# The causal mask of one attention sublayer, added in blocks of 32 queries

## The reference

```python
q = (x @ Wq + bq).reshape(B, T, H, D).transpose(0, 2, 1, 3)
k = x @ Wk + bk
v = x @ Wv + bv
q = apply_rope(q)
k = apply_rope(k)
att = jnp.einsum('bhqd,bkd->bhqk', q, k) / jnp.sqrt(jnp.float32(D))
causal = jnp.tril(jnp.ones((T, T), dtype=bool))
att = jnp.where(causal[None, None], att, jnp.float32(-jnp.inf))
att = jax.nn.softmax(att, axis=-1)
out = jnp.einsum('bhqk,bkd->bhqd', att, v)
out = out.transpose(0, 2, 1, 3).reshape(B, T, C)
return out @ Wo + bo
```

## Time and profile before

| what | value |
|---|---|
| median of three runs | 1877.55 us (1872.98 to 1877.91) |
| the profiled execution | 1875.85 us |
| its span in the trace | 1874.1 us |
| TensorE busy over the span | 1541.5 us |
| DVE, ScalarE, GpSimd busy | 1112.2, 875.0, 611.7 us |

### The profile page before, as it was taken

The page is one execution under the profiler, slowest core; times in us unless marked ns, Lnnn a source line. Parts: engine busy times, 40 slices in busy tenths (PEclk is TensorE's granted clock), DMA queues, the critical chain, the costliest instruction groups (busy, mean ns, idle before and its releaser), DMA issues.

```text
span 1874.1 us, 42923 instructions
## 1 busy us (share of the span) xinstructions
PE 1541.5 (82%) x15916; PEld 1011.6 (54%) x15916; DVE 1112.2 (59%) x3614; ACT 875.0 (47%) x2556; POOL 611.7 (33%) x849
## 2 busy tenths in 40 slices
PE   4556379979989778898889633799799999998998
PEld 3334246546656555455557422566477777776443
DVE  3434555556757557116757687466566666664776
ACT  2222334445556335434546544344366666666443
POOL 1422231222226434002212243112144444443666
PEclk6555569989999889999989855799899999999999
DMA  5000000000000000000020000000000000000000
GB/s 229 2 1 2 1 1 2 2 1 2 2 2 2 1 0 1 1 1 2 2 117 3 24 1 1 1 2 2 24 1 1 0 0 0 0 0 1 1 12 12
DMA packets 3605, 21.53 MB, mean 11 GB/s; under 512 B 1129, under 2 KB 1385, under 8 KB 2025
## 3 DMA queue, kind: packets, MB, share of 16 engines
q1 hardware_dynamic: 3434, 19.22, 2.7%
HBM read 18.15 MB, written 1.05 MB: 10 GB/s over the span
## 4 chain that ended last, share of the span: by engine, by line
PE 67%; DVE 11%; issue 7%; ACT 6%; POOL 4%; DVEq 3%; POOLq 1%; DMA 0%; ACTq 0%; SPq 0%
PE ps L707 5%; PE ps L646 5%; PE ps L675 5%; PE ps L2829 4%; PE ps L2478 4%; PE ps L2488 3%; PE ps L2502 3%; PE ps L2457 3%; PE ps L2464 3%; PE ps L606 2%; PE ps L717 2%; PE ps L2301 2%; PE ps L1264 2%; PE ps L662 2%; PE ps L694 2%
## 5 line engine op out<-in xcount | busy, mean ns | idle before, releaser
L894 DVE TENSOR_REDUCE arena<-ps 128x4 f32<-128x512 f32 x320 | 204.3, 684 | 132.5 <-PE ps L662 74.8
L832 ACT ACTIVATE arena<-ps 128x512 f32<-128x512 f32 x320 | 171.7, 596 | 126.6 <-PE ps L694 124.2
L537 POOL TENSOR_TENSOR arena<-arena,C 128x512 f32<-128x512 f32 x80 | 83.2, 1041 | 420.2 <-ACT arena L853 138.6
L2394 POOL TENSOR_TENSOR arena<-arena 128x512 f32<-128x512 f32 x128 | 132.9, 1044 | 224.2 <-DVE arena L2703 223.8
L1264 PE MATMUL ps<-hid,WA 128*20 128x16 f32 x1024 | 56.8, 196 | 88.0 <-DVE hid L1315 88.0
L2621 ACT COPY arena<-ps 128x512 f32<-128x512 f32 x128 | 69.1, 589 | 122.9 <-PE ps L2488 122.9
L2612 ACT ACTIVATE arena<-ps,arena 128x256 f32<-128x256 f32 x256 | 120.1, 479 | 11.8 <-issue 8.1
L2829 PE MATMUL ps<-WA,maskadd 128*128 128x512 f32 x256 | 119.8, 598 | 1.8 <-DVE arena L2972 1.8
L707 PE MATMUL ps<-arena 128*32 128x128 f32 x2560 | 110.9, 282 | 3.3 <-ACT arena L832 3.0
L646 PE MATMUL ps<-arena 32*128 32x128 f32 x2560 | 104.1, 288 | 9.9 <-POOL arena L537 6.8
L2695 DVE TENSOR_REDUCE arena<-ps 128x2 f32<-128x512 f32 x128 | 82.5, 686 | 45.0 <-PE ps L2478 43.5
(11 more groups left out here) (455 smaller groups left out, 3847.8 us busy)
## 6 DMA issues: line engine op xcount, KB each, us to landing
WA<-w_late SPq DMA_DIRECT2D x1, 4228.0 KB, 13.7
WA<-w_early SPq DMA_DIRECT2D x1, 1600.0 KB
R<-rows SPq DMA_DIRECT2D x1, 1282.0 KB, 6.8
WB<-w_rest SPq DMA_DIRECT2D x1, 1152.0 KB, 10.1
xT_all<-x_T SPq DMA_DIRECT2D x1, 1024.0 KB, 6.4
x_all<-x_tok SPq DMA_DIRECT2D x1, 1024.0 KB, 12.2
arena<-mask SPq DMA_DIRECT2D x1, 1024.0 KB
ctxT_all<-ctx_T SPq DMA_DIRECT2D x1, 1024.0 KB
```

The costliest lines, as they stand in the source:

```text
L537: nc.gpsimd.tensor_tensor(heads(v_(n % 2, ATT, "P", WIDE_Q, 512)), src.unsqueeze(1).broadcast_to([128, 4, 128]), cst("tilemask").unsqueeze ...
L832: nc.scalar.activation(v_(s, ATT, "PT", 512 * t, 512), ps[s][t][:, :], ACT.Exp, scale=SCALE).then_inc(pT_sb, 1)
L894: nc.vector.tensor_reduce(v_(z, ATT, "m", 4 * t, 4), heads(ps[z][t][:, :]), AXX, ALU.max)
L2394: nc.gpsimd.tensor_tensor(p, p, v_(z, LAT, "rec", 4 * u + 2 * x, 2).unsqueeze(2).broadcast_to([128, 2, 256]), ALU.mult).then_inc(l_sub, 1)
```

## The change

For `mask_kind == "causal"` the mask is added by products of 32 rows instead of 128. Two new tiles, `causal_4` and `ident_4`, hold the mask and the identity so that each group of 32 rows of the array has all four blocks of 32 queries. They are filled by 32 transfers on SyncE's queue from `causal_b` and `ident_b`, after the last load. In `scores`, block b covers the keys from 32 b on. The order of blocks is outside and that of row groups inside, and `s_ps` is incremented in block 3. In `scores_T`, block b covers the 32 queries of the block for all keys.

```diff
+        causal_4 = sb("causal_4", [128, 4, 128], BF16)
+        ident_4 = sb("ident_4", [128, 4, 128], BF16)
...
+        const_cast = sem("const_cast")
+        fours_in = sem("fours_in")
...
+                elif mask_kind == "causal":
+                    if n == 0:
+                        pe.wait_ge(fours_in, 512)
+                    for b in range(4):
+                        for t in ORDER:
+                            mm = nc.tensor.matmul(heads(ps[z][t][:, :])[:, :, 32 * b:128], ident_4[rows(t), b, :],
+                                                  causal_4[rows(t), b, 32 * b:128].unsqueeze(1).broadcast_to(
+                                                      [32, 4, 128 - 32 * b]), start=False, stop=b == 3,
+                                                  skip_group_check=True)
+                            if b == 3:
+                                mm.then_inc(s_ps, 1)
                 elif mask_kind is not None:
                     for t in ORDER:
-                        r = (maskadd[:, n:n + 1, :].broadcast_to([128, 4, 128])
-                             if mask_kind == "full" else causal_b[:, :].unsqueeze(1).broadcast_to([128, 4, 128]))
-                        nc.tensor.matmul(heads(ps[z][t][:, :]), ident_b[:, :], r, start=False, stop=True,
+                        nc.tensor.matmul(heads(ps[z][t][:, :]), ident_b[:, :],
+                                         maskadd[:, n:n + 1, :].broadcast_to([128, 4, 128]), start=False, stop=True,
                                          skip_group_check=True).then_inc(s_ps, 1)
...
+                elif mask_kind == "causal":
+                    for b in range(4):
+                        for t in T_ORDER:
+                            nc.tensor.matmul(heads(ps[s][t][:, :])[:, :, 32 * b:32 * b + 32], causal_4[rows(t), b, :],
+                                             ident_b[rows(t), rows(t)].unsqueeze(1).broadcast_to([32, 4, 32]),
+                                             start=False, stop=False, skip_group_check=True)
                 elif mask_kind is not None:
-                    l = causal_b[:, :] if mask_kind == "causal" else maskadd[:, n, :]
                     for t in T_ORDER:
-                        nc.tensor.matmul(heads(ps[s][t][:, :]), l,
+                        nc.tensor.matmul(heads(ps[s][t][:, :]), maskadd[:, n, :],
                                          ident_b[:, :].unsqueeze(1).broadcast_to([128, 4, 128]), start=False,
                                          stop=False, skip_group_check=True)
...
+            sp.wait_ge(const_cast, 1)
+            for t in range(4):
+                for b in range(4):
+                    to, of = slice(32 * t, 32 * t + 32), slice(32 * b, 32 * b + 32)
+                    sp.dma_start(causal_4[to, b, :], causal_b[of, :]).then_inc(fours_in, 16)
+                    sp.dma_start(ident_4[to, b, :], ident_b[of, :]).then_inc(fours_in, 16)
...
-            nc.vector.tensor_copy(negrow_b[:, :], cst("second").broadcast_to([128, REG_ROWS]))
+            nc.vector.tensor_copy(negrow_b[:, :], cst("second").broadcast_to([128, REG_ROWS])).then_inc(const_cast, 1)
```

## The result

The changed kernel takes 1858.89 us, the median of 4 runs (1855.54 to 1860.48), where the kernel before takes 1875.65 us (1872.98 to 1877.91). The ratio is 0.9906, with a 95% interval of 0.9893 to 0.9919: 16.8 us less. The profiled execution took 1860.04 us, its span is 1858.1 us. The functions of the sublayer stand some lines lower in this file: scores L650 (was L646), their mask L667 (L662), transposed scores L689 (L675), their mask L699 (L685), fold L713 (L694), values L726 (L707), maxima L913 (L894), rope L903 (L884), widening L541 (L537).

A forecast was written before the change was run, and what follows sets the result against it. TensorE was taken to bound the causal sublayer until a loop through DVE and POOL closes at 7.41 us. Savings of 14 x 1.07 + 1.0 + 0.8 = 16.8 us from 1877.55 gave 1861 us, range 1856 to 1870.

The forecast's parts named there:

- TensorE bounds the stage, until a loop closes: Causal sublayer: TensorE busy for all of 118.00 us, so every us taken from it counts until another loop closes.
- Transposed scores, 1.22 us in place of 2.04: TensorE's transposed scores with their mask, per sequence: 0.97 + 0.25 = 1.22 us, a saving of 0.82.
- Scores, 1.75 in place of 2.07: TensorE's scores with their mask, per sequence: 0.97 + 0.78 = 1.75 us, a saving of 0.32.
- The loop of 7.41 us: Causal step through TensorE, DVE and POOL: 1.72 + 3.24 + 0.04 + 2.37 + 0.04 = 7.41 us, setting the step.
- The stall of 0.07 us ahead of L646: TensorE waits 0.07 us before the next scores, as the loop of 7.41 exceeds its own step of 7.34.
- First sequence 1.0, last 0.8: Savings at the causal sublayer's ends: 1.0 us in the first sequence, 0.8 in the last.
- The transfers cost nothing: 32 transfers of 8 KB on SP after the last weight load: at most 38 us of SP, no added time.
- All before 1188 us where it was: Changed profile: everything ahead of the causal sublayer unmoved, everything behind it 17 us earlier.
- row groups that don't run side by side: Rival for the causal masks: row groups fail to overlap, +1.2 us a step, 1897 us; chance 0.04.
- a fixed price of 0.06 us per product: Rival: 16 narrow products cost 0.97 us like four wide ones, only mode changes saved, 1874 us; chance 0.04.
- The longer loop: Rival: another loop binds in the causal step at 7.6 to 7.9 us, giving 1866 to 1870 us; chance 0.22.
- The clock elsewhere: Rival: work behind the sublayer meets clock changes at other moments, eating most of the gain, 1872 us; chance 0.05.

The follow-up runs named there:

- halves of the change: Kernel before with narrow products for one mask only: scores' mask alone 1869.55 us, transposed scores' mask alone 1862.02 us.
- the early normalisation: Changed kernel with DVE's normalisation of sequence k - 2 moved ahead of the first two maxima of k + 1, causal sublayer alone: 1856.76 us.
- the second profile: Changed kernel run and profiled once more, nothing altered, beside the kernel before: 1857.99 us, ratio 0.9904.

## Why the prediction was right

The forecast of 16.8 us less is met by the medians (16.8). Step by step:

- *TensorE bounds the stage, until a loop closes.* Right. The halves of the change each come off in full on TensorE, 0.43 and 0.85 us a step.
- *Transposed scores, 1.22 us in place of 2.04.* 1.19 in the trace. L694 was the right row for the price.
- *Scores, 1.75 in place of 2.07.* Mis-sized: 1.64. The term that failed is "512 columns (L655) and twice 128 (half of L694)" per group. L694 has 8 products in the earlier trace rows because the fold is done for two banks there, so two groups stream four times 128 columns, and the other two nothing. The 0.57 us hold 1024 columns, 0.43 us, and 0.14 of ends, not 0.25. With that the sum is 0.97 + 0.53 + 0.14 = 1.64. TensorE's own step is 7.19, not 7.34; the early normalisation shows it bare.
- *The loop of 7.41 us.* Its parts were right: first maximum at 0.75 (0.74), maxima to cut 3.24 (1245.80 to 1249.04), rope to widening 2.37. The hop of 0.04 between cut and rope was wrong in sign. Rope waits for nothing and starts at 1248.96, 0.08 ahead of the end of the record before it. So the loop is 7.31, and the step 7.31 in place of 7.41. Over 14 steps 0.10 would be 1.4 us more than the sum's 15.0. Measured are 15.97, since the first of these steps gives less: it was 7.95 us long already before and is 7.07 after.
- *The stall of 0.07 us ahead of L646.* It is 0.11 to 0.12, and it ends with POOL's L541 as said. Both of its terms were off, TensorE's by 0.15 and the loop's by 0.10, so its size was near by luck.
- *First sequence 1.0, last 0.8.* 1.78 and 0.85. Both depend on the moments at which the clock changes: in the second profile of the same kernel the first is 10.98 - 9.87 = 1.11, and the last sequence takes 1312.25 - 1299.73 = 12.52 us there, 0.50 less than before, with a granted clock of 0.67 in its last 3.25 us.
- *The transfers cost nothing.* Shown within the interval, 1.0001 (0.9992 to 1.001).
- *All before 1188 us where it was.* Wrong for the profiled execution, by 2.63 us, through the clock in earlier sublayers. Without it the profile would have lain 18.6 us lower.

That the medians agree with the forecast to a tenth is luck. The stage itself gave 18.6 us in the first profile and 142.02 - 124.36 = 17.7 in the second, 0.9 to 1.8 more than the 16.8 of the sum, and the interval of the ratio, 0.9893 to 0.9919, spans 15 to 20 us. The forecast time of 1861 lies 2.1 us above the measured 1858.89, since it starts from the median of three runs, 1877.55, which with a fourth run is 1875.65.

The rivals: row groups that don't run side by side and a fixed price of 0.06 us per product are excluded by 0.23 us for 16 products. The longer loop was the right kind of mechanism, but at 7.31 it costs 1.5 us in all, not 5 to 9. The clock elsewhere moved single profiles as that rival said: ahead of the sublayer by the 2.2 us above, and behind it, where 543.4 us follow the last output product in the kernel before and in the changed kernel's first profile, and 541.2 in its second. There the granted clock from 1338 to 1348 us is 1.00; in the same part of the program it is 0.87 before (1356 to 1366) and in the first profile (1340 to 1350). It didn't eat most of the gain.

## What to carry to other kernels

A mask added by a product costs the columns streamed per row group, whatever is in them, as long as the products aren't too many (64 of 32 columns took 0.51 us, 16 of 128 columns 0.23). Put the mask, not the identity, into the weights, so that only the 32 columns of a block per head are streamed, and let the four row groups work on four banks: 0.23 us did what 0.97 did on the transposed scores, 0.33 on the scores. Then look at who waits for the last product and not for the first: the increments moved to the end of the mask here, and the loop began to bind. It had had 1.4 us to spare: by the rows of before it is 1.53 + 3.24 - 0.08 + 2.37 + 0.05 = 7.1 us (an estimate), in a step of 8.48.

Busy time of an engine near 100% says that it bounds only if no wait stands in the step. In the causal sublayer there was none, and the saving came off in full. In the linear one there was a wait of 0.2 us for DVE; it grew, and of the 0.44 us saved at the mask none was left in the step.

## What the runs showed of the hardware that was not expected

Products for different row groups start out of program order: with all blocks of one group ahead of the next group in the program, the four groups still begin within 0.1 us, and both masks take what they took (0.22 and 0.68 us against 0.23 and 0.65). The Trainium skill ("TensorE: Matmul & The Clock Gate", "What overlaps and what doesn't", in "The mechanism" of Part 3) says that matmuls start and end strictly in program order. For the starts the trace differs, and decides.

Starts of narrow products over four row groups come as close as 8 ns (64 in 0.51 us). The floor of about 25 ns that the same page gives ("Wait — 56ns, not 53.3ns?") can then hold only within a row group, where 32 ns were seen.

The moment at which the granted clock rises differs between executions of one program by enough to move a sublayer by 3.4 us (1187.89 and 1191.32). A comparison of single traces needs the stage's own length and not its place in the span.
